# Attention scores from two float16 parts, with two heads in the two 64-row halves of the array

## What is computed

```python
h = tokens(x)                        # frames -> |DFT|^2 -> mel -> log -> DCT -> 192 numbers per frame
z = layernorm(h)
q, k, v = z @ V_Q @ U_Q + bias_q, z @ V_K @ U_K + bias_k, z @ V_V @ U_V + bias_v      # 12 heads of 16
attn = softmax(((q @ M_U) @ (M_V @ k.T)) / sqrt(16))                                  # 750 x 750 per head
h = h + attn @ v
return h + experts(layernorm(h))
```

## Time and profile before

| | |
|---|---|
| median of 3 runs | 3539.42 us (3538.19 to 3545.73) |
| span of the profiled execution | 3519.2 us |
| PE busy | 92% of the span |
| DVE busy | 61% |
| ACT busy | 47% |
| chain that ended last | PE 71%, DVE 13%, ACT 6%, issue 6% |

### The profile page before, as it was taken

How to read it: one execution, slowest core, us unless ns; L and a number is a source line. 1 busy time by engine, 2 the same in 40 slices (tenths; PEclk the granted TensorE clock), 3 DMA queues, 4 the chain that set the end, 5 groups by cost and what they waited for, 6 DMA issues and landing times.

```text
span 3519.2 us, 63111 instructions
## 1 busy us (share of the span) xinstructions
PE 3240.1 (92%) x22736; PEld 1851.1 (53%) x22736; DVE 2153.8 (61%) x3828; ACT 1665.5 (47%) x2403; POOL 629.2 (18%) x1097
## 2 busy tenths in 40 slices
PE   6979999999989899998989999899999989999987
PEld 3544455554646555464545546455554645555555
DVE  3228666766657566665756666565766656667545
ACT  1134645545454554545455454544545454554542
POOL 1520120303012120301212030120303012110201
PEclk8578989998999989899998989899998989999889
DMA  5333321202121220212222031222202122121000
GB/s 123 105 105 88 82 36 54 54 14 76 30 69 31 62 43 15 76 31 63 35 62 43 14 76 30 61 36 63 45 14 76 31 60 37 56 44 25 8 7 7
DMA packets 146247, 174.99 MB, mean 50 GB/s; under 512 B 30081, under 2 KB 134874, under 8 KB 143950
## 3 DMA queue, kind: packets, MB, share of 16 engines
q1 hardware_dynamic: 143772, 163.37, 19.3%
q0 software_dynamic: 1280, 7.08, 0.9%
q10 hardware_dynamic: 898, 0.47, 0.1%
HBM read 105.49 MB, written 64.51 MB: 48 GB/s over the span
## 4 chain that ended last, share of the span: by engine, by line
PE 71%; DVE 13%; ACT 6%; issue 6%; DMA 2%; POOL 1%; SPq 1%; ACTq 0%; DVEq 0%; POOLq 0%
PE ps L1109 68%; DVE negm L920 7%; ACT big L738 2%; DVE st L864 1%; PE ps L1195 1%; ACT hn L703 1%; PE ps L1278 1%; ACT rest L670 1%; ACT parts L686 1%; DVE mres L928 1%; POOL h0t L493 0%; DVE mvr L870 0%; DVE onrm L951 0%; DMA qs<-in_w 0%; PE ps L1147 0%
## 5 line engine op out<-in xcount | busy, mean ns | idle before, releaser
L920 DVE TENSOR_REDUCE negm<-ps 125x1 f32<-125x750 f32 x1152 | 1065.3, 934 | 672.2 <-PE ps L1109 662.6
L738 ACT ACTIVATE big<-ps 125x750 f32<-125x750 f32 x1152 | 906.4, 793 | 821.1 <-PE ps L1109 817.6
L1109 PE MATMUL ps<-ks,qs 96*125 96x375 bf16 x2304 | 632.1, 359 | 92.9 <-issue 37.8
L1109 PE MATMUL ps<-qs,ks 99*125 99x375 bf16 x2304 | 660.9, 371 | 55.7 <-DVE negm L920 46.5
L1109 PE MATMUL ps<-big,V 125*32 125x188 f32 (+1 forms) x9216 | 629.8, 355 | 5.3 <-DVE onrm L951 2.6
L1109 PEld LDWEIGHTS ps<-qs,ks 99*125 99x125 bf16 x2304 | 245.3, 144 | 417.4 <-issue 237.4
L1024 DVE SCALAR_TENSOR_TENSOR rest<-ps,fb,h1s 128x375 f32<-128x375 f32 (+1 forms) x448 | 251.7, 603 | 320.4 <-PE ps L1109 315.3
L1109 PEld LDWEIGHTS ps<-ks,qs 96*125 96x125 bf16 x2304 | 310.9, 149 | 257.4 <-issue 118.6
L493 POOL TENSOR_TENSOR h0t<-h0t,onrm 125x384 f32<-125x384 f32 x48 | 48.0, 1001 | 1863.7 <-DVE onrm L951 1863.4
L1109 PEld LDWEIGHTS ps<-big,V 125*32 125x32 f32 x9216 | 201.1, 112 | 334.7 <-issue 326.7
L752 ACT ACTIVATE h1s<-ps,fb,wsc 128x375 f32<-128x375 f32 (+1 forms) x448 | 272.0, 657 | 213.8 <-PE ps L1109 213.8
(11 more groups left out here) (173 smaller groups left out, 3327.8 us busy)
## 6 DMA issues: line engine op xcount, KB each, us to landing
qs<-qk_scratch SPq DMA_DIRECT2D x288, 93.8 KB, 3.5
ks<-qk_scratch SPq DMA_DIRECT2D x288, 93.8 KB, 4.4
qk_scratch<-parts SPq DMA_DIRECT2D x32, 562.5 KB, 4.7
v_scratch<-vtmp SPq DMA_DIRECT2D x16, 1125.0 KB
V<-v_scratch SPq DMA_DIRECT2D x48, 375.0 KB
h_scratch<-h0t SPq DMA_DIRECT2D x16, 562.5 KB
hn<-h_scratch SPq DMA_DIRECT2D x16, 562.5 KB
h0t<-h_scratch SPq DMA_DIRECT2D x16, 562.5 KB
```

The lines of the kernel that those rows point to most:

```text
L738: nc.scalar.activation(halves(probs[:, i % 2, h, :]), slot(s, TP), ACT.Exp).then_inc(exp_done, 1)
L920: V_.tensor_reduce(negm[:, n:n + 1], slot(s, TP), axis=AX.XY, op=MAX, negate=True).then_inc(max_done, 1)
L1109: return nc.tensor.matmul(o, l, r, start=start, stop=stop)
```

## The change

Queries and keys are split into two float16 parts, and three products of parts are summed instead of six: a head then needs 48 partitions (KROWS), and two more for the maxima, which have two parts instead of three. Two heads fit above each other: one at partitions 0 to 49, one at 64 to 113. An A or B tile keeps its two matmuls of 375 columns, but the two are now two heads in the two 64-row halves of the array, each writing one bank of the slot, where they were two column halves of one head on 96 or 99 rows. The compiled program has these matmuls at row positions 0 and 64 with tiles of 64 x 128; PV stays in four strips of 32 columns, all others use the whole array.

To keep float16 in range, the query and key weights are scaled by powers of two found at setup, the constant rows hold 32768, and the exponential takes its scale from a column of wsc. The reduction gives two maxima per partition (negp, 125 x 2), and max_parts joins the two column halves first. The raw copy and the third part are gone: ACT casts the first part straight out of PSUM, DVE subtracts it from the same PSUM slot and writes the second part, and the slot is free when DVE is done (parts_ready). Stacks move in the same 12 transfers per group with half the bytes; the maxima take four transfers instead of three. The staging buffers of the expert weights (wst) no longer share memory with qs.

```diff
-QPARTS = ((0, 3, 0), (3, 2, 1), (5, 1, 2))
-KPARTS = ((0, 3), (3, 2), (5, 1))
+QPARTS = (0, 0, 1)
+KPARTS = (0, 1, 0)
+SLOTS = len(QPARTS)
 KROWS = SLOTS * D
-MROWS = 3
+MROWS = 2
...
-            return (raw_ready, 4 * m + k - 1) if k < 6 else (v_ready, 3 * m + k - 5)
+            return (parts_ready, 4 * m + k - 1) if k < 6 else (v_ready, 3 * m + k - 5)
...
             store_parts(0)
-            sp.wait_ge(w_split, 4)
             store_v(0)
+            sp.wait_ge(setup_dve, 1)
...
-                    nc.scalar.activation(halves(probs[:, i % 2, h, :]), slot(s, TP), ACT.Exp).then_inc(exp_done, 1)
+                    nc.scalar.activation(probs[:, i % 2, 2 * c:2 * c + 2, HC * n:HC * n + HC], slot(s, TP), ACT.Exp,
+                                         scale=wsc[0:TP, 21:22]).then_inc(exp_done, 1)
...
-                V_.tensor_tensor(r_, r_, parts[0:rows, t, 0, :], op=SUB).then_inc(rest_ready, 1)
+                V_.tensor_tensor(lo, slot(s, rows), hi, op=SUB).then_inc(parts_ready, 1)
...
-                V_.tensor_reduce(negm[:, n:n + 1], slot(s, TP), axis=AX.XY, op=MAX, negate=True).then_inc(max_done, 1)
+                V_.tensor_reduce(negp[:, 2 * n:2 * n + 2], slot(s, TP), axis=AX.X, op=MAX, negate=True).then_inc(max_done, 1)
...
-                h, j = n // J, n % J
+                c, j, n2 = n // (2 * J), n % (2 * J) // 2, n % 2
                 for q in range(2):
-                    ins = mm(slot(s, TP)[:, q, :], qs[0:KROWS, g, NF * h + TP * j:NF * h + TP * j + TP],
-                             ks[0:KROWS, g, NF * h + HC * q:NF * h + HC * q + HC])
+                    r = slice(64 * q, 64 * q + KROWS)
+                    ins = mm(slot(s, TP)[:, q, :], qs[r, g, NF * c + TP * j:NF * c + TP * j + TP],
+                             ks[r, g, NF * c + HC * n2:NF * c + HC * n2 + HC])
                 ins.then_inc(a_done, 1)
...
-                K = KROWS + MROWS
+                i, n, c = k // HG, k % HG // HP, k % HP
                 for q in range(2):
-                    ins = mm(slot(s, TP)[:, q, :], ks[0:K, g, NF * h + TP * i:NF * h + TP * i + TP],
-                             qs[0:K, g, NF * h + HC * q:NF * h + HC * q + HC])
+                    r = slice(64 * q, 64 * q + KROWS + MROWS)
+                    ins = mm(slot(s, TP)[:, q, :], ks[r, g, NF * c + TP * i:NF * c + TP * i + TP],
+                             qs[r, g, NF * c + HC * n:NF * c + HC * n + HC])
                 ins.then_inc(b_done, 1)
```

More of the change, by code:

```diff
@@ L134, in build @@
         hn2 = sb("hn2", [TP, J, 256], fp32)
[L135 to L137 removed]
+        qs = sb("qs", [128, G3, HP * NF], fp16)
+        ks = sb("ks", [128, G3, HP * NF], fp16)
+        parts = sb("parts", [128, 4, 2, NF], fp16)
         rest = sb("rest", [128, 2, NF], fp32)
@@ L208, in build @@
         scratch = parts[:].rearrange("p t c n -> p (t c n)").bitcast(fp32)
-        wst = [qs[:].rearrange("p g c -> p (g c)").bitcast(fp32)[:, 2 * NFF * i:2 * NFF * i + 2 * NFF] for i in range(2)]
+        sel_s = hn2[0:4 * NE1].rearrange("p j e -> p (j e)")[:, 0:CH * 128]
+        wst = [wst0[:], wst1[:]]
         def tmp(rows, n):
@@ L379, in load_stacks @@
                 h0 = g * HG * D
[L380 to L387, removed]
+                for i, (stack, order) in enumerate(((ks, KPARTS), (qs, QPARTS))):
+                    for q in range(2):
+                        for s, part in enumerate(order):
+                            src = qk_dram[bass.ds(m, 1), 1 - i, part, h0:h0 + HG * D, :].rearrange("o (c r d) t -> (o r) d c t", r=2, d=D)[q]
+                            dst = stack[64 * q + D * s:64 * q + D * s + D, g, :].rearrange("p (c t) -> p c t", c=HP)
+                            sp.dma_start(dst, src).then_inc(stacks_loaded[g], 16)
                 if g == 0:
@@ L396, in load_maxrows @@
                 sp.wait_ge(mT_ready, 3 * m + g + 1)
-                for c in range(3):
-                    dst = qs[KROWS + c:KROWS + c + 1, g, :].rearrange("o (r t) -> o r t", r=TILES)
-                    sp.dma_start(dst, mTs[TILES * c:TILES * c + TILES, :]).then_inc(maxrows_loaded[g], 16)
+                for q in range(2):
+                    for c in range(MROWS):
+                        r0, n = TILES * c + HP * J * q, HP * J
+                        dst = qs[64 * q + KROWS + c:64 * q + KROWS + c + 1, g, :].rearrange("o (r t) -> o r t", r=n)
+                        sp.dma_start(dst, mTs[r0:r0 + n, :]).then_inc(maxrows_loaded[g], 16)
             def store_y(m):
@@ L513, in pre_norm @@
                 ins.then_inc(ln1_ready, 1)
[L515 to L519, removed]
             def fold(dst, src, n):
@@ L668, in pre_tile @@
                     act.wait_ge(proj_done, 7 * m + t + 1)
-                    wait(act, parts_ready, 4 * m + t - 1)
-                    nc.scalar.activation(halves(rest[0:rows, t % 2, :]), slot(s, rows), ACT.Copy).then_inc(raw_ready, 1)
                     if t == 0:
                         wait(act, parts_stored, 64 * m)
-                    act.wait_ge(raw_ready, 4 * m + t + 1)
-                    nc.scalar.activation(parts[0:rows, t, 0, :], rest[0:rows, t % 2, :], ACT.Copy).then_inc(part1_ready, 1)
+                    nc.scalar.activation(halves(parts[0:rows, t, 0, :]), slot(s, rows), ACT.Copy).then_inc(part1_ready, 1)
                 else:
@@ L681, in pre_tile @@
                     nc.scalar.activation(vtmp[:, 2 * q:2 * q + 2, :, 0:D], src, ACT.Copy).then_inc(v_ready, 1)
[L683 to L686, removed]
             def prep_tile(m, i, s):
@@ L752, in ffn @@
                         ins = nc.scalar.activation(h1s[0:rows, u % 2, s, :], ps[0:rows, s, 0:HC], ACT.Identity,
-                                                   bias=fb[0:rows, 2, s * CH + c:s * CH + c + 1], scale=wsc[0:rows, 8:9])
+                                                   bias=fb[0:rows, 2, s * CH + c:s * CH + c + 1], scale=wsc[0:rows, 17:18])
                     ins.then_inc(h1_copied, 1)
@@ L840, in scales @@
+                V_.tensor_scalar(fb[:, 2, :], fb[:, 0, :], wsc[:, 14:15], None, MUL)
+                V_.tensor_scalar(fb[:, 3, :], fb[:, 1, :], wsc[:, 16:17], None, MUL).then_inc(scales_ready, 1)
+                for k, w in enumerate((wq, wk)):
+                    V_.tensor_scalar(w[:, 0, :], w[:, 0, :], wsc[:, 18 + k:19 + k], None, MUL)
+                    V_.tensor_scalar(w[0:65, 1, :], w[0:65, 1, :], wsc[0:65, 18 + k:19 + k], None, MUL).then_inc(qk_scaled, 1)
                 for half in range(2):
@@ L909, in _, with pre_rest @@
                 copy_h0(B - 2 + q, q, 16 * (B // 2 - 1))
-            def pre_rest(m, t):
+            def pre_rest(m, t, s):
                 rows = 128 if t % 2 == 0 else E - 128
-                r_ = rest[0:rows, t % 2, :]
                 dve.wait_ge(part1_ready, 4 * m + t + 1)
-                V_.tensor_tensor(r_, r_, parts[0:rows, t, 0, :], op=SUB).then_inc(rest_ready, 1)
+                hi, lo = (parts[0:rows, t, c, :].rearrange("p (n c) -> p n c", n=2) for c in range(2))
+                V_.tensor_tensor(lo, slot(s, rows), hi, op=SUB).then_inc(parts_ready, 1)
             def amax(a, s, n):
                 dve.wait_ge(a_done, a + 1)
-                V_.tensor_reduce(negm[:, n:n + 1], slot(s, TP), axis=AX.XY, op=MAX, negate=True).then_inc(max_done, 1)
+                V_.tensor_reduce(negp[:, 2 * n:2 * n + 2], slot(s, TP), axis=AX.X, op=MAX, negate=True).then_inc(max_done, 1)
             def max_parts(G):
@@ L1014, in att @@
                         if ("P", 0, 2) in tiles and t is not None:
-                            pre_rest(b + 2, t)
+                            pre_rest(b + 2, t, dict(in_slot(tiles))[("P", t + 2, 2)])
             def swiglu(m, u):
@@ L1083, in _ @@
                 if kind == "P" and 3 <= k < 7:
-                    pre_rest(tile[2], k - 3)
+                    pre_rest(tile[2], k - 3, (s - 1) % 3)
                 if kind == "P" and k == 2 and tile[2] == 0:
```

92 lines of the change are left out of this document (47 added, 45 removed).

## The result

The changed kernel takes 3855.99 us (median of 4 runs, 3826.79 to 3864.74) against 3539.78 beside it: a ratio of 1.0865, interval 1.0818 to 1.0912. The sign was forecast, the size was not: +316 us where I said +131. The page of the changed kernel has these lines for PE, the reduction and the exponential; the last column is the idle time before them and what ended it.

What follows compares the result with a forecast made beforehand. PE sets the 1.24 us step. Loop samples +127, samples 0, 1, 14, 15 +67, ahead of sample 0 −13, clock rises −48: +133 on 3519.2, 3652; with runs' median 20 higher, 3670 stated. Range 3415 to 3750.

Steps and rivals of the forecast that it cites:

- The step at 0.50: Plain attention step at half clock: overlapping halves of A and B shorten it from 2.23 to 1.65 us.
- The step at 1.00: Plain attention step at full clock: overlapping halves of A and B shorten it from 1.24 to 0.95 us.
- g0 and g1: Attention groups g0, g1: run at half clock until the FFN, +5.5 us a period, or +13.5 without a gate drop before.
- What raised it is gone: Group starts, steps 2 to 5: PE now waits for DVE's 0.85 us reductions, so the clock no longer rises there.
- 1.00 in most of g1: Sign in group g1 of the changed trace: full clock in most of it would make the forecast wrong.
- the sum: Whole kernel: +127 us for loop samples, +67 for samples 0, 1, 14, 15, −13 ahead of sample 0, −48 for clock rises.
- g2: Attention group behind the FFN: stays at full clock, +0.3 us net, including 0 to 5.6 of waits for P-tile slots.
- dip at its DVE-paced start: Start of group g2: one more dip in clock, priced at +1.5 us.
- Mode changes: A and B against transposes and P tiles: about 24 new array-mode changes a period at 0.15 us, g2's third +1.0.
- Ahead of sample 0: Before the first sample: PE's waits for a slot (7.85 us) and stacks (2.91) shrink; −8 to −15, taken as −13.
- The clock holds: Rival: group starts still raise the clock; −7.5 us a period, about −125 in all, 3415 us; chance 0.25.
- The halves run one after the other: Rival for A and B: steps and clock unchanged, mode changes cost 3.6 us a period, about 3575 us; chance 0.08.

Runs made afterwards that it cites:

- e9: Changed kernel with queries' and keys' P tiles copied raw by ACT to free the slot early, plus twelve useless matmuls per gate: 3458.39 us, 0.9767 of the kernel before.
- e8: Changed kernel with a tile's two heads at the same rows, run serially, zero-padded to 96 and 98 rows, slots still late: 3513.95 us, 0.9874 of the kernel before.
- e5: Kernel before, with the P-tile slot of queries and keys held until DVE's subtraction instead of ACT's raw copy: 3696.98 us, ratio 1.0464.
- e2: Changed kernel with queries' and keys' P tiles copied raw by ACT, freeing the slot early, and split from the copy: 3566.31 us, 1.0045 of the kernel before.
- e4: Changed kernel with every A and B tile of the attention steps computed twice into the same slot: 3665.07 us.
- e1b: Changed kernel with a tile's two heads side by side in columns at the same rows 0 to 49, so their matmuls run serially: 4516.05 us.
- e10: Changed kernel with a tile's two heads at the same rows, run serially, zero-padded to 66 and 68 rows in whole-array mode: 4349.84 us.

## Why the prediction was wrong

**The step at 0.50: right.** Forecast 1.65; B to B in g0 of the changed kernel is 1.61, and B to A is 0.37 where it was 0.68. A whole stream of 0.31 left each tile, so the halves overlap fully. The estimate that I worked out from the Trainium skill ("TensorE: Matmul & The Clock Gate", Part 3), a step near 1.85, is not borne out.

```profile
1373.63 0.57 PE L1105 MATMUL ps<-qs,ks 50*125 50x375 f16 x2
...
1374.00 0.52 PE L1105 MATMUL ps<-ks,qs 48*125 48x375 f16 x2
...
1375.24 0.57 PE L1105 MATMUL ps<-qs,ks 50*125 50x375 f16 x2
```

**The step at 1.00: mis-sized.** Forecast 0.95. In e9, which has it in all of g1, B to B is 0.92 where the tiles wait for nothing (1434.43 to 1435.35), but 1.08 on the mean of twelve steps (1426.66 to 1439.65):

```profile
1426.66 0.38 PE L1108 MATMUL ps<-qs,ks 50*125 50x375 f16 x2 [0.56 <-DVE negp L919]
...
1431.31 0.89 ACT L725 ACTIVATE big<-ps,wsc 125x750 f32<-125x750 f32 x1 [0.24 <-PE ps L1108]
...
1434.43 0.38 PE L1108 MATMUL ps<-qs,ks 50*125 50x375 f16 x2
...
1435.35 0.37 PE L1108 MATMUL ps<-qs,ks 50*125 50x375 f16 x2
...
1439.65 0.37 PE L1108 MATMUL ps<-qs,ks 50*125 50x375 f16 x2
```

PE no longer sets it alone: tiles wait for DVE or ACT here and there. The exponential takes 886 ns instead of 793, the up to 0.1 that I had allowed for the scale column and the strided output and then put at nothing; which of the two it is, no run separates.

**g0 and g1: the mechanism right, too strong.** "What raised it is gone" held for the start of g0, and g0 takes 46.7 against a forecast of 48.5. But behind the F transposes, to which I had given one sample in four, the clock rose in every sample of the loop, and the gate dropped it again (1363.6 and 1370.4 in the sample shown). PE waits for DVE at the start of a group as said (0.41 for the reduction, with A and B 0.36 apart):

```profile
1341.04 0.57 PE L1105 MATMUL ps<-ks,qs 48*125 48x375 f16 x2
1341.40 0.52 PE L1105 MATMUL ps<-qs,ks 50*125 50x375 f16 x2
...
1342.65 0.57 PE L1105 MATMUL ps<-qs,ks 50*125 50x375 f16 x2 [0.41 <-DVE negp L916]
```

But g1 took the cold 41 to 43 us in only four of the twelve samples and 33 in eight, in which the clock rose some 9 us after its start. By my own sign, "1.00 in most of g1", the forecast for g1 was wrong. Together g0 and g1 cost +2.9 a period, where I had +5.5 or +13.5. That samples 0, 1, 14 and 15 add 62, beside the +67 of the sum, is luck: the sum had most of it in g0 and g1, the trace has 48 of it in FFN and g2.

**g2: the step that failed.** "It stays at 1.00, being full of P tiles behind the FFN", +0.3, and +2.8 with the FFN; measured +20.6. I had seen that the slot would be held longer and put 0 to 5.6 us on it as time that PE waits. That range held: the waits are about 1 us each, and with the clock held FFN and g2 take 1.2 more (e8). What I left out was to ask of g2 the question that I had asked of g0 and g1, what a wait does to the clock in a kernel whose plain steps stream half as much. Nor was g2 at 1.00 before: the earlier trace rows has 0.97 ahead of the loop's branch. The runs show that it takes both: the late slot with full streams costs 1.2 (e8) or, held longer still, 9 (e5); half the streams with an early slot cost nothing in g2 in eleven of twelve samples (e2); together they cost 20.6, and 6.7 when the streams alone are given back (e4). My "dip at its DVE-paced start" was priced as one dip of 1.5; in the g2 shown the clock fell behind two P tiles (1274.8 and 1291.9), the second time to the end of g2.

**Mode changes: right in size, and no cause of the loss.** At 0.50, B to the P tile behind it is 0.82 in e1b, whose B tiles lie in a 64-row half, and 0.68 in e10, whose B tiles are in whole-array mode (2003.56 to 2004.24 above):

```profile
2012.04 0.89 PE L1106 MATMUL ps<-qs,ks 50*125 50x375 f16 x2
...
2012.86 1.62 PE L1106 MATMUL ps<-xA,wq 128*128 128x375 f32 x2
```

The 0.14 between them is near the 0.15 that I had taken. And e2, which keeps all the mode changes, is within 0.5% of the kernel before.

**Ahead of sample 0: right inside, hidden by something else.** PE's twelve transposes of the first P tile and its first A tile:

```profile
207.52 2.76 PE L1192 MATMUL ps<-idf,hn 125*128 125x125 f32 x12 [1.45 <-DVE h0t L852]
...
254.74 1.02 PE L1105 MATMUL ps<-ks,qs 48*125 48x375 f16 x6
```

From the one to the other it is 47.2 us, and was 60.5 (198.53 to 258.98): the 13 us forecast. But the transposes come 9 us later than before. About 8 of them lie in the setup, where DVE now finds and applies the powers of two of the query and key weights ahead of a copy out of PSUM for which PE waits; the copy, before and after:

```profile
92.42 0.94 DVE L850 COPY big<-ps 100x750 f32<-100x750 f32 x1
...
100.47 0.94 DVE L846 COPY big<-ps 100x750 f32<-100x750 f32 x1
```

**The rivals.** "The clock holds" got its point of decision half right: the clock still rose in most samples of g1. What it gives when it holds, 7.5 us a period in the forecast, is 7.6 in e9 (204.7 to 197.1), but that is luck: e9 has no fall behind the gate, which the rival had kept, and g0, g1 and FFN with g2 give 1.7, 4.0 and 1.9. Its sum has a slip: 16 times 7.5 and 13 make 133, not 125. "The halves run one after the other" is out by the rows above.

## What to carry to other kernels

A matmul that does the same work in half the streaming time is not simply faster where the granted clock falls in thinly streamed stretches, as it does here: price the step at both levels of the clock, and ask of every wait in the stretch, old or new, whether it will now drop it. A PSUM slot should go free at the first copy out of it; to let a second engine read it too saved an ACT pass here and cost 290 us (with the clock held, in e8, 1.2 us a period). Where the clock falls at a known thin place, a few useless full-array matmuls put there can be worth more than they take: 12 in each gate brought about 100 us (e9 against e2, 0.9767 against 1.0045 of the kernel before).

## What the runs showed of the hardware

In these runs the granted clock went not only with when PE streams but with how many rows its matmuls fill. With the same columns at the same spacing, scores of 48 and 50 rows gave a mean clock of 0.670 and 4516 us, 66 and 68 rows 0.686 and 4350 us, 96 and 98 rows, half of them zeros on one side, 0.925 and 3514 us. So padding a short contraction with rows of zeros took 22% off the time of a kernel that computes the same numbers. And the two matmuls in the two 64-row halves overlapped wholly: a pair of 375 columns took the time of one (0.37 us from B to A at 0.50, where it was 0.68 and a stream is 0.31).
